# Query projections of four heads packed into three blocks of 128 rows, and routing weights turned on VectorE

## The reference

```python
x = x + xattn(layernorm(x), ctx_768, Wq, Wk, Wv, Wo, bo)
#   q = xn @ Wq, k = ctx @ Wk, v = ctx @ Wv, per head of 64
#   softmax(q k^T / 8) v, heads joined, @ Wo + bo
x = x + ffn(layernorm(x), ...)
#   scores = sigmoid(tokens @ router.T); + bias; best 2 of 4 groups; best 4 experts
#   w = 2.5 * scores[top4] / sum;  out = sum_e w_e * down_e(silu(gate_e t) * up_e t) + shared
```

## Time and profile before

| what | value |
|---|---|
| median of 3 runs | 3230.2 us (3229.17 to 3230.35) |
| profiled execution | 3230.45 us |
| its span, first to last instruction | 3228.5 us |
| TensorE busy | 3192.1 us, 99% |
| VectorE busy | 2387.4 us, 74% |
| ScalarE busy | 2022.8 us, 63% |
| GpSimd busy | 1333.5 us, 41% |

### The profile page before, as it was taken

One profiled execution on the slowest core, in us unless ns is written; L12 is line 12 of the kernel. 1 busy time (PEld: TensorE's weight loads), 2 busy tenths in 40 slices (PEclk: granted clock), 3 DMA queues, 4 the chain that ended last, 5 costly groups with the idle time before them and its releaser, 6 DMA issues.

```text
span 3228.5 us, 40831 instructions
## 1 busy us (share of the span) xinstructions
PE 3192.1 (99%) x15150; PEld 2544.2 (79%) x15150; DVE 2387.4 (74%) x4866; ACT 2022.8 (63%) x2364; POOL 1333.5 (41%) x894
## 2 busy tenths in 40 slices
PE   7999999999999999999999999999999999999999
PEld 6777777778777777778777777777777778777787
DVE  5777777777777777777777777777777777777766
ACT  4666666666666666666666666666666666676555
POOL 5333433344333444334433344333443334225565
PEclk9999999999999999999999999999999999999999
DMA  2000000000000000000000000000000000105553
GB/s 82 1 17 1 17 1 1 17 1 17 1 17 1 17 1 1 17 1 17 1 17 1 17 1 17 1 1 17 1 17 1 17 1 1 40 3 128 119 128 76
DMA packets 26971, 67.49 MB, mean 21 GB/s; under 512 B 3347, under 2 KB 4628, under 8 KB 26388
## 3 DMA queue, kind: packets, MB, share of 16 engines
q1 hardware_dynamic: 26772, 64.87, 7.7%
HBM read 61.72 MB, written 2.62 MB: 20 GB/s over the span
## 4 chain that ended last, share of the span: by engine, by line
PE 96%; DVE 1%; POOL 1%; issue 1%; ACT 0%; DMA 0%; POOLq 0%; SPq 0%; DVEq 0%; ACTq 0%
PE st L586 12%; PE st L589 12%; PE side L528 11%; PE op L599 11%; PE op L605 11%; PE op L602 11%; PE st L592 11%; PE side L622 3%; PE st L720 2%; PE st L722 2%; PE st L721 2%; PE side L521 1%; PE op L613 1%; PE op L616 1%; PE side L523 1%; PE side L522 1%
## 5 line engine op out<-in xcount | busy, mean ns | idle before, releaser
L466 POOL TENSOR_TENSOR p_lo<-p_full,p_hi 128x1024 fp32r<-128x1024 f32 x320 | 819.8, 2562 | 1754.5 <-ACT p_hi L895 1754.5
L1174 DVE TENSOR_REDUCE m_part<-side 128x1 f32<-128x400 f32 x2016 | 1074.4, 570 | 502.9 <-PE side L528 502.8
L892 ACT ACTIVATE p_full<-st 128x1024 f32<-128x1024 f32 x768 | 789.2, 1028 | 877.9 <-PE st L592 846.6
L895 ACT ACTIVATE p_hi<-st 128x1024 fp32r<-128x1024 f32 x768 | 785.0, 1022 | 0.0
L1157 DVE TENSOR_TENSOR p_lo<-p_full,p_hi 128x1024 fp32r<-128x1024 f32 x448 | 546.0, 1219 | 85.1 <-ACT p_hi L895 85.1
L528 PE MATMUL side<-cT_hi,qT_hi 96*128 96x400 f32 x2016 | 554.8, 346 | 0.0
L586 PE MATMUL st<-qT_hi,cT_hi 97*128 97x512 f32 x1664 | 541.7, 406 | 8.7 <-DMA qT_hi<-m_row 7.8
L589 PE MATMUL st<-qT_lo,cT_hi 96*128 96x512 f32 x1664 | 524.3, 396 | 0.0
L599 PE MATMUL op<-p_hi,v_hi 128*97 128x512 f32 x1536 | 487.0, 398 | 1.6 <-DVE p_lo L1157 1.6
L602 PE MATMUL op<-p_lo,v_hi 128*97 128x512 f32 x1536 | 481.1, 394 | 0.0
L605 PE MATMUL op<-p_hi,v_lo 128*97 128x512 f32 x1536 | 481.1, 394 | 0.0
(11 more groups left out here) (173 smaller groups left out, 3097.7 us busy)
## 6 DMA issues: line engine op xcount, KB each, us to landing
w_rep<-w_rows SPq DMA_DIRECT2D x64, 512.0 KB, 6.5
keys_nat<-in_ctx_keys SPq DMA_DIRECT2D x16, 672.0 KB, 6.0
keys_tur<-in_ctx_turned SPq DMA_DIRECT2D x16, 600.4 KB, 4.8
gud_raw<-in_moe_w SPq DMA_DIRECT2D x2, 1152.0 KB, 7.7
out_x<-x SPq DMA_DIRECT2D x8, 256.0 KB, 2.0
x<-in_x SPq DMA_DIRECT2D x1, 1920.0 KB, 13.5
qT_hi<-m_row SPq DMA_DIRECT2D x64, 4.0 KB
oT<-e_row SPq DMA_DIRECT2D x64, 4.0 KB
```

Source lines behind the costliest of these rows:

```text
L466: pool.tensor_tensor(p_lo[:, slot(s), :], p_full[:, s % 2, :], p_hi[:, slot(s), :].bitcast(F32), ALU.subtract).then_inc(s_lo_pool, 1)
L892: act.activation(p_full[0:m, s % 2, :], made, ACT.Exp, scale=SCALE)
L895: act.activation(p_hi[0:m, slot(s), :], made, ACT.Exp, scale=SCALE).then_inc(s_ex, 1)
L1174: dve.tensor_reduce(m_part[:, k % NT, k // NT:k // NT + 1], where[:, 0:MAXW], AX.X, ALU.max).then_inc(s_drain, 1)
```

## The change

- `A_hi`, `A_lo`, `A_raw` of four heads are three blocks of 128 columns instead of four of 96: blocks 0 and 1 and 2 hold heads 0, 1, 2 in columns 0 to 95, and the fourth head lies in thirds of 32 in columns 96 to 127 of each. `stacked` gives the three copies that fill them.
- `project_queries` runs three blocks by three matmuls in place of four heads by three. The first job makes blocks 0 and 1, the second block 2. `unstacked` gives the pieces in which ScalarE and VectorE copy the result out: three for the first job, two for the second; the fourth head's thirds come from partitions 96 to 127 and go to partitions 0, 32 and 64.
- In `PLACES` the second query job moves behind the weighing of tile 10, on all three engines; on ScalarE its copies come after the exponentials of the half tile, on VectorE its low part comes after `early_steps` and the half tile's low part.
- `route_weights` turns a batch's weights with a VectorE transpose of 32x32 blocks into `w_turned`; `turn_routing` on TensorE, `keep_routing` on ScalarE and their semaphores go, also the wait for `s_wk` in the last group. SyncE stores each batch with four DMAs, from the last group of a batch on, ahead of the row of maxima, and the last three batches after the attention.

```diff
-        A_hi = sb(att, "A_hi", [P, H, DC], F32R)
+        A_hi = sb(att, "A_hi", [P, NGB, 3, P], F32R)
...
-                  12: ("QQ", "")}
+                  12: ("Q", "Q")}
...
+        DT = DC // 3
+
+        def stacked(tile, n, banks):
+
+            return [(tile[:, n, 0:2, 0:DC], banks[:, :, 0:DC]),
+                    (tile[:, n, 2, 0:DC], banks[:, 0, DC:2 * DC]),
+                    (tile[:, n, :, DC:P], banks[:, 1, DC:2 * DC].rearrange("p (k m) -> p k m", k=3))]
+
+        def unstacked(tile, where, k):
+
+            last = slice(3 * NQ, GQ)
+            if k == 0:
+                return [(tile[0:DC, 0:BANK], where[0:DC, :]),
+                        (tile[0:DT, last], where[DC:P, 0:NQ]),
+                        (tile[DT:2 * DT, last], where[DC:P, NQ:BANK])]
+            return [(tile[0:DC, BANK:3 * NQ], where[0:DC, 0:NQ]),
+                    (tile[2 * DT:DC, last], where[DC:P, 0:NQ])]
...
-            def store_routing(c):
-                sp.wait_ge(s_wk, c + 1)
-                sp.dma_start(w_rows[c], wT[:, c % 2, :]).then_inc(s_wd, 16)
+            def store_routing(batch):
+
+                sp.wait_ge(s_rw, batch + 1)
+                c, first = batch // 2, batch % 2 * 2 * P
+                for run in range(4):
+                    rows = w_rows[c, :, first:first + 2 * P].rearrange("e (t r j) -> e t r j", t=2, r=4)
+                    sp.dma_start(rows[:, :, run, :],
+                                 w_turned[run * E:(run + 1) * E, batch % 2, :].rearrange("e (t j) -> e t j", t=2)).then_inc(s_wd, 16)
...
                 else:
+                    if i == NGB - 1 and b >= 2:
+                        store_routing(b - 2)
                     send_max_row(jobs_at(g)["T"][0] + 1, (i + 1) % 2)
...
-                for h in range(2):
-                    head = g * GH + 2 * k + h
-                    o = where[0:DC, h * NQ:(h + 1) * NQ]
-                    pe.matmul(o, A_hi[:, head, :], x_hi[:, half, :], start=True, stop=False)
-                    pe.matmul(o, A_hi[:, head, :], x_lo[:, half, :], start=False, stop=False)
-                    mm = pe.matmul(o, A_lo[:, head, :], x_hi[:, half, :], start=False, stop=True)
+                for block in ((0, 1), (2,))[k]:
+                    o = where[:, block % 2 * NQ:(block % 2 + 1) * NQ]
+                    pe.matmul(o, A_hi[:, g, block, :], x_hi[:, half, :], start=True, stop=False)
+                    pe.matmul(o, A_hi[:, g, block, :], x_lo[:, half, :], start=False, stop=False)
+                    mm = pe.matmul(o, A_lo[:, g, block, :], x_hi[:, half, :], start=False, stop=True)
...
-            def turn_routing(c, where):
...
-                act.activation(qT_hi[slot][0:DC, k * BANK:(k + 1) * BANK], where[0:DC, :], ACT.Copy).then_inc(s_qh, 1)
+                for into, made in unstacked(qT_hi[slot], where, k):
+                    ins = act.activation(into, made, ACT.Copy)
+                ins.then_inc(s_qh, 1)
...
-                for k, j in enumerate(place["Q"]):
+                for k, j in enumerate(place["Q"][:1]):
                     queries_hi(bank(j), j + 1, k, i % 2)
                 exp(FULL)
+                for k, j in enumerate(place["Q"][1:], 1):
+                    queries_hi(bank(j), j + 1, k, i % 2)
...
-                dve.tensor_tensor(qT_lo[slot][:, cols], where[0:DC, :], qT_hi[slot][0:DC, cols].bitcast(F32),
-                                  ALU.subtract).then_inc(s_drain, 1)
+                high = unstacked(qT_hi[slot], where, k)
+                for (into, made), (kept, _) in zip(unstacked(qT_lo[slot], where, k), high):
+                    ins = dve.tensor_tensor(into, made, kept.bitcast(F32), ALU.subtract)
+                ins.then_inc(s_drain, 1)
...
+                if batch >= 0:
+                    if batch >= 2:
+                        dve.wait_ge(s_wd, 64 * (batch - 1))
+                    dve.transpose(w_turned[:, batch % 2, :], w_new[:, :]).then_inc(s_rw, 1)
```

More of the change, by code:

```diff
@@ L356, in _ @@
                         store_output(c - 1)
+                if c == 1:
+                    store_routing(B - 2)
+                    store_routing(B - 1)
             for c in (NCH - 2, NCH - 1):
@@ L432, in _ @@
             for c in (2, 3):
-                heads = slice(4 * c, 4 * c + 4)
                 pool.wait_ge(s_abk, c)
-                pool.tensor_tensor(A_lo[:, heads, :], A_raw[:, heads, :], A_hi[:, heads, :].bitcast(F32),
+                pool.tensor_tensor(A_lo[:, c, :, :], A_raw[:, c, :, :], A_hi[:, c, :, :].bitcast(F32),
                                    ALU.subtract).then_inc(s_Ap, 1)
@@ L624, in project_head @@
                 mm.then_inc(s_fill, 1)
-            def turn_routing(c, where):
-                for t in range(4):
-                    mm = pe.transpose(where[0:E, t * P:(t + 1) * P], w_all[:, 4 + c * 4 + t, :], ident[:, :])
-                mm.then_inc(s_wf, 1)
             def body(b, i, g):
@@ L690, in body @@
                     pv(t - 2)
-                    if g == NG - 1 and t == 2:
-                        pe.wait_ge(s_drain, first_job[g])
-                        pe.wait_ge(s_rw, B)
-                        turn_routing(0, bank(first_job[g] + 1))
                     side_jobs(at[t][1])
@@ L782, in _ @@
                         turn_output(c - 1)
-                    if q == 2 and c + 1 < NCH:
-                        if c:
-                            pe.wait_ge(s_wk, c)
-                        else:
-                            pe.wait_ge(s_drain, JOBS_END)
-                        if c + 1 == NCH - 1:
-                            pe.wait_ge(s_rw, B + 2)
-                        turn_routing(c + 1, side[:, (c + 1) % 2, :])
             for g in range(NCH * NP - 3, NCH * NP):
@@ L821, in keep_products @@
                     act.wait_ge(s_ab, 2 * n + 2)
-                    act.activation(four_heads(A_raw, n), products(banks, slice(0, 2 * DC)), ACT.Copy)
-                    act.activation(four_heads(A_hi, n), products(banks, slice(0, 2 * DC)), ACT.Copy)
+                    for tile in (A_raw, A_hi):
+                        for into, made in stacked(tile, n, banks):
+                            act.activation(into, made, ACT.Copy)
                 b = B_all[0:DC, 4 * n:4 * n + 4, 0:D].rearrange("p (c j) m -> p j c m", c=2)
@@ L829, in _ @@
             act.wait_ge(s_ab, 2)
-            act.activation(four_heads(A_hi, 0), products(op, slice(0, 2 * DC)), ACT.Copy).then_inc(s_xh, 1)
+            for into, made in stacked(A_hi, 0, op):
+                ins = act.activation(into, made, ACT.Copy)
+            ins.then_inc(s_xh, 1)
             act.wait_ge(s_tur, 16)
@@ L866, in x2_hi_of @@
                                ACT.Copy).then_inc(s_xxh, 1)
-            def keep_routing(c, where):
-                act.wait_ge(s_wf, c + 1)
-                if c >= 2:
-                    act.wait_ge(s_wd, 16 * (c - 1))
-                act.activation(wT[:, c % 2, :], where[0:E, :], ACT.Copy).then_inc(s_wk, 1)
             def body(b, i, g):
@@ L913, in body @@
                         x2_hi_of(0)
-                    if g == NG - 1 and s == 3:
-                        keep_routing(0, bank(first_job[g] + 1))
                     extra = EXTRA.get(i, {}).get(s)
@@ L966, in _ @@
                         hidden_hi(g - 1)
-                    if q == 3 and c + 1 < NCH:
-                        keep_routing(c + 1, side[:, (c + 1) % 2, :])
                     if g == 10:
@@ L1098, in strike, with route_weights @@
                 link(ins)
-            def route_weights(tiles):
+            def route_weights(batch):
                 link(dve.tensor_tensor(ra[:, :, :], struck[:, :, 0:E], choice[:, :, 0:E], ALU.not_equal))
@@ L1106, in route_weights @@
                 share = r1[:, :].rearrange("p (a b) -> p a b", b=1).to_broadcast([P, 2, E])
-                dve.scalar_tensor_tensor(w_all[:, tiles, :], ra[:, :, :], ROUTE_SCALE, share, ALU.mult,
-                                         ALU.mult).then_inc(s_rw, 1)
+                link(dve.scalar_tensor_tensor(w_new[:, :].rearrange("p (t e) -> p t e", t=2), ra[:, :, :], ROUTE_SCALE,
+                                              share, ALU.mult, ALU.mult))
+                if batch >= 0:
+                    if batch >= 2:
+                        dve.wait_ge(s_wd, 64 * (batch - 1))
+                    dve.transpose(w_turned[:, batch % 2, :], w_new[:, :]).then_inc(s_rw, 1)
             dve.memset(m_part[:, :, :], 0.0)
@@ L1118, in _ @@
             dve.wait_ge(s_xh, 2)
-            first = A_hi[:, 0:4, :].rearrange("p (c j) m -> p j c m", c=2)
-            dve.tensor_tensor(A_lo[:, 0:4, :].rearrange("p (c j) m -> p j c m", c=2),
-                              op[:, :, 0:2 * DC].rearrange("p j (c m) -> p j c m", c=2), first.bitcast(F32),
-                              ALU.subtract).then_inc(s_Al, 1)
+            for (into, made), (kept, _) in zip(stacked(A_lo, 0, op), stacked(A_hi, 0, op)):
```

(2 more changed lines are left out.)

30 lines of the change are left out of this document (11 added, 19 removed).

## The result

The changed kernel takes 3263.35 us (median of four runs, 3262.68 to 3265.32); the kernel before took 3230.27 beside it (3229.17 to 3230.55). The ratio is 1.0109, with a 95% interval of 1.0097 to 1.0121. The profiled execution has a span of 3260.9 us, 32.4 more than before, at the same granted clock, 0.997. The forecast was 3257.

A forecast was written before the change was run, and what follows sets the result against it. The ScalarE and VectorE chain at group boundaries was taken as the bound. Boundaries 26.2 + weighing 1.6 + turned routing 0.7 + start 0.4 + routing transposes 0.6 - 2.6 = 26.9 us, giving 3257 us, +0.8%, range 3229 to 3267.

The forecast's parts named there:

- What bounds the kernel: At group boundaries the chain through ScalarE and VectorE ends with TensorE, which can give back at most 0.17 us each.
- ScalarE's copies: First query job's three copies at a boundary don't overlap: over at 2.47 us, half tile's first exponential at 2.50.
- VectorE's low parts: Three low parts at a boundary, each followed by a 0.03 gap: next step starts at 4.10 us, 0.71 late.
- first rival: Query pieces overlap as today's do, VectorE's next step only 0.27 us late: 3231 us, no change; chance 0.13.
- third kind: Boundary at 1082.06, once per batch: half tile's low part 0.25 us late, next scores 0.08 us later.
- The boundaries: Four kinds, each once per batch: next group's scores later by 1.69 us per batch, 26.2 us over 15.5 batches.
- The weighing: Next group's first tile: its weighing waits some 0.1 us 16 times, 1.6 us; turned routing adds 0.7 us.
- second kind: Boundary at 1036.98, once per batch: half tile's low part 0.71 us late, next scores 0.66 us later.
- Routing: Removed TensorE transposes gain 2.6 us, two VectorE transposes cost 0.6 us; SyncE's four stores per batch are hidden.
- Start: Weight products go through three ScalarE copies instead of one, for two tiles, ahead of GpSimd's work: 0.4 us.
- The sign that failed: If the forecast was right, TensorE busy time would fall by some 25 us while the span grows.
- boundary without query jobs: Boundary at 2877: TensorE has 1.4 us less to do, yet the scores start 7.72 us after the low half's copy.

The follow-up runs named there:

- e: Kernel before with three low products of the second query job's matmuls left out, nine query matmuls per group instead of twelve: 3225.38 us, ratio 0.9988.
- f: Changed kernel with as many query pieces of as many columns, all read from and written to partition 0, fourth head wrong: 3225.98 us, ratio 0.9991.
- j: Changed kernel with only VectorE's query pieces at partition 0, ScalarE's copies keeping their partitions, fourth head wrong: 3240.18 us, ratio 1.0034.
- a: Kernel before with the second query job moved as in the change, and nothing else: 3231.71 us, ratio 1.0006.
- b: Kernel before with the routing weights turned on VectorE and stored batch by batch, queries as they were: 3226.22 us, ratio 0.9991.

## Why the prediction came out right, and where it was off

**What bounds the kernel.** Right. In e, TensorE lost a quarter of its query matmuls and the kernel gained 4 us of 22.

**ScalarE's copies.** Forecast: over at 2.47, first exponential at 2.50. They were over at 2.43, and it started at 2.45. The price of a piece of 32x256, taken from a tile of 128x256, held. The groups by form, after:

```profile
L1024 DVE TENSOR_TENSOR qT_lo<-side,qT_hi 32x256 fp32r<-32x256 f32 x192 | 81.9, 426 | 2.6
L817 ACT ACTIVATE qT_hi<-side 32x256 fp32r<-32x256 f32 x192 | 72.7, 379 | 2.2
...
L1112 DVE STREAM_TRANSPOSE w_turned<-w_new 128x64 f32<-128x64 f32 x16 | 3.9, 245 | 0.6
```

**VectorE's low parts.** Forecast: the next step starts at 4.10, with 0.417 for each 32x256. It started at 4.06, with 0.426: the pieces follow each other with a gap of 0.014, not 0.03. That a shifted piece follows with a gap and not with an overlap, the step on which forecast and first rival parted, is shown by f and j. The rule that the prediction takes from the Trainium skill (VectorE: DVE Perf Modes, section on two Vector instructions with no wait between them) agrees with both. The Trainium skill's overlap of some 93 ns between ACTIVATEs (ScalarE: Activation LUTs, What ACT_TABLE_LOAD costs) agrees with f's copies, which overlap by 0.10, and not with those of the change (1.12 and 1.38 us for the three).

One row shows that on VectorE the change of start partitions against the last read costs even where the instruction itself moves nothing between partitions. In the third kind of boundary the step behind the pieces is striking: MEMSETs, which read nothing, and then a MATCH_VALUE_LOAD (L1096), which moves nothing to other partitions. Before, and in f and j, it starts 0.05 us behind the end of the MEMSET of `best` and beside a MEMSET of `spare`; in the change it starts 0.14 behind it, when the MEMSET of `spare` has ended. It is the first to read since the shifted pieces. The whole step takes 0.64 us in the change and 0.54 in the three others. For ScalarE the two causes were not separated.

**The boundaries.** Forecast for the low part: late by 0.54, 0.71, 0.25, 0.71; measured 0.51, 0.68, 0.34, 0.68. For the scores: 0.37, 0.66, 0.08, 0.58, sum 1.69; measured 0.36, 0.63, 0.16, 0.56, sum 1.71. Over 15.5 batches that is 26.5 us, forecast 26.2. That the sums agree so well has some luck in it: the third kind is twice the forecast, because the striking step took 0.10 longer, and VectorE's shorter gaps make up for it in all.

**The weighing.** Forecast 1.6 us for the second kind and 0.7 for the turned routing, on the way from the scores to the first tile's weighing. That way grew more: from 1.77, 1.82, 1.76 and 1.77 to 1.86, 2.01, 1.87 and 1.86, together 0.48 per batch or 7.4 us. Some 0.09 of it stands in every kind, where VectorE has its low part ready. I had missed this term. It is TensorE's start after a wait: the first pair of score matmuls takes 0.73 us, and its weight load starts together with it; a pair that waits for nothing takes 0.63, with its weights loaded 0.23 ahead. In the earlier trace rows the pair without a wait has 0.63, in the earlier trace rows the one behind a wait 0.73. Over 62 boundaries 0.09 is 5.6 us; the remaining 1.9 answers to the forecast 2.3. The experiments bear it out: in e, where ScalarE and VectorE do what they did before and only TensorE comes to wait, the way is 1.86 or 1.87 in all four kinds, in f too, and in a, where TensorE doesn't wait, it is 1.75 to 1.77. The row to read it from was in hand: I priced the wait and not the restart behind it.

**Routing.** Forecast 2.6 us gained and 0.6 lost, two net. Measured 3.1 behind attention, and 2.9 in b, where the routing is changed alone. The transpose takes 0.245, forecast 0.25. SyncE's four stores issue in 2.08 us, 10.6 ahead of the row of maxima; they are hidden, as the queue of the changed kernel shows:

```profile
1126.93 2.08 SPq L334 DMA_DIRECT2D w_rows<-w_turned  x4
1137.53 0.64 SPq L312 DMA_DIRECT2D qT_hi<-m_row  x1
```

**Start.** Forecast 0.4 us, measured 1.8. This is the term that was mis-sized most. I counted the copies of the weight products and left out that the first group's queries go through the same pieces, and with no attention beside them. ScalarE's five copies and VectorE's five low parts stand in the serial start:

```profile
11.86 2.17 ACT L817 ACTIVATE qT_hi<-side 96x512 fp32r<-96x512 f32 x5 [0.72 <-PE side L547]
13.27 2.46 DVE L1024 TENSOR_TENSOR qT_lo<-side,qT_hi 96x512 fp32r<-96x512 f32 x5 [3.15 <-ACT qT_hi L817]
```

The last copy ends at 14.03 instead of 13.36. VectorE's last low part ends at 15.73 instead of 14.08, and its first maxima start at 15.76 instead of 14.49. GpSimd's part of the products (A_lo) then starts at 23.39 instead of 21.88. The copies of the products add 0.24 of these 1.51.

**The sum.** Measured: 26.5 (boundaries) + 1.9 (weighing) + 5.6 (restart) + 1.8 (start) - 3.1 (routing) = 32.7; the last group and roundings make the 32.4 of the span. Forecast: 26.9. The difference of 5.5 is as large as the restart, 5.6; start (1.4 more than forecast) and routing (1.1 more gained) were off in opposite directions and nearly cancel, which is luck.

**The sign that failed.** I wrote that TensorE's busy time would fall by some 25 us; it fell by 7.4, though the matmuls are gone. The row counts the modelled ends of matmuls: behind a pair of 0.63 the next starts after 0.46, so each idle stretch lets 0.17 of an end count that was covered before, and the pair behind it counts 0.10 more. 62 x 0.27 is 16.7, nearly the 17.6 that are missing. This was worked out and not tried. The share of the chain (96% to 81%) and the wait's own row are the signs to read.

## What to carry to other kernels

Before taking work off an engine that is 99% busy, look for a place in the trace where that work is already missing, and see how far the next step moved: here the boundary without query jobs gave 0.17 us for 1.4 us less work. When blocks are packed so that a matmul fills its rows, count the pieces that carry them out again, and count a piece that changes partitions at its full duration plus a gap, on each engine that runs it; here the change of partitions cost 37 us and the matmuls saved gave 4. And where a cut on TensorE turns into a wait, add its restart behind the wait, 0.09 us each here.

## What the runs showed of the hardware

ScalarE pays for a change of start partitions as VectorE does: three copies take 1.38 us with it and 1.12 without, and a follower starts 0.01 behind the end instead of 0.10 ahead of it. VectorE's starts 0.014 behind instead of 0.08 ahead. A piece of 32 partitions costs what 128 partitions cost (0.426 against 0.417 us on VectorE, 0.379 against 0.386 on ScalarE). TensorE lost 0.09 us more than the wait itself at each stop ahead of its 512-column score matmuls; there the weight load starts with the first matmul and not 0.23 ahead of it. No version that packs the queries and computes all four heads right was faster than routing alone (b, 3226.2 us); f, which doesn't, took 3226.0.
